# Graph attention and eight experts on one core: the first expert's first layer for all tokens, and expert blocks between the last graph loads

## What is computed

```python
x = x + gnn(layernorm(x), edges, ...)   # two attention layers over a graph: 8 heads of 768, then 1 head
h = layernorm(x)
probs = softmax(h @ Wg + bg)            # 8 experts
comb = one_hot(argmax(probs)) * max(probs)
y_e = gelu(h @ W1[e] + b1[e]) @ W2[e] + b2[e]      # 768 -> 3072 -> 768, for each e
ffn = sum_e comb[:, e] * y_e
v = clip(ffn @ Wv + bv, -3, 3)
scores = sigmoid(h @ Wm + bm); mask = scores >= 12th largest
gr, gi = diagonal of a complex tridiagonal inverse of v (two recursions over the tokens)
out = x + ffn + bk_scale * (clip([gr, gi] * mask) @ Wo + bo)
```

## Time and profile before

| | |
|---|---|
| runs | 503.71, 502.79, 503.6 us, median 503.6 |
| profiled execution, its own time | 506.07 us |
| its span in the trace | 504.3 us |
| granted TensorE clock, mean | 0.99 |
| busy TensorE / VectorE / ScalarE / GpSimd | 92% / 27% / 12% / 7% |
| bytes moved | 190.22 MB, mean 377 GB/s |

### The profile page before, as it was taken

One profiled execution on the slowest core, in us unless ns is written; L12 is line 12 of the kernel. 1 busy time (PEld: TensorE's weight loads), 2 busy tenths in 40 slices (PEclk: granted clock), 3 DMA queues, 4 the chain that ended last, 5 costly groups with the idle time before them and its releaser, 6 DMA issues.

```text
span 504.3 us, 6062 instructions
## 1 busy us (share of the span) xinstructions
PE 466.4 (92%) x2310; PEld 232.4 (46%) x2310; DVE 137.0 (27%) x362; ACT 60.6 (12%) x113; POOL 33.9 (7%) x52
## 2 busy tenths in 40 slices
PE   7999998999999999999999999998898889789892
PEld 5656665667558344344344353352243224224352
DVE  6573698426206311010010010020010002001165
ACT  1110212002003020021020020110020011002100
POOL 3262240000000000210000000000000000000000
PEclk9999999999999999999999999999999999999996
DMA  8889998898999999999999999999999999999700
GB/s 309 305 301 402 401 400 297 307 407 323 411 357 369 417 425 423 414 423 423 423 429 423 422 428 427 420 423 430 423 423 426 427 422 423 427 423 424 297 1 31
DMA packets 32541, 190.22 MB, mean 377 GB/s; under 512 B 5423, under 2 KB 5631, under 8 KB 18190
## 3 DMA queue, kind: packets, MB, share of 16 engines
q1 hardware_dynamic: 31694, 189.94, 92.6%
q0 software_dynamic: 544, 0.05, 0.1%
q10 hardware_dynamic: 288, 0.03, 0.0%
HBM read 189.62 MB, written 0.39 MB: 377 GB/s over the span
## 4 chain that ended last, share of the span: by engine, by line
PE 60%; SPq 16%; DMA 15%; DVE 5%; issue 2%; ACT 1%; POOL 0%; DVEq 0%
PE ps L1286 17%; PE ps L1259 16%; PE ps L1081 11%; SPq L337 8%; DMA chunk<-in_L_ffn_W 7%; DMA lower<-in_L_ffn_W 6%; PE ps L1041 6%; SPq L316 4%; SPq L332 3%; PE ps L1272 2%; PE ps L1069 2%; DMA slot<-in_L_gnn_W 2%; PE ps L1096 2%; PE ps L1221 2%; SPq L354 1%
## 5 line engine op out<-in xcount | busy, mean ns | idle before, releaser
L1286 PE MATMUL ps<-lower,hidden 128*64 128x384 f32 x600 | 102.9, 491 | 6.1 <-DMA lower<-in_L_ffn_W 6.1
L1259 PE MATMUL ps<-chunk,gathered 128*64 128x512 f32 x408 | 92.6, 597 | 10.0 <-DMA chunk<-in_L_ffn_W 10.0
L1286 PEld LDWEIGHTS ps<-lower,hidden 128*64 128x64 f32 x600 | 41.3, 136 | 58.3 <-issue 45.1
L1041 PE MATMUL ps<-slot,xT 128*128 128x384 f32 x192 | 64.1, 488 | 1.2 <-DMA slot<-in_L_gnn_W 1.2
L1259 PEld LDWEIGHTS ps<-chunk,gathered 128*64 128x64 f32 x408 | 27.5, 136 | 66.9 <-issue 47.6
L1081 PE MATMUL ps<-slot,eluT 128*128 128x384 f32 x168 | 55.3, 486 | 0.0
L866 DVE TENSOR_TENSOR biased<-ps,b_T 128x384 f32<-128x384 f32 x32 | 17.1, 554 | 133.5 <-PE ps L1272 133.5
L1041 PEld LDWEIGHTS ps<-slot,xT 128*128 128x128 f32 x192 | 35.6, 190 | 23.9 <-issue 1.3
L1259 PE MATMUL ps<-extra,gathered 128*64 128x512 f32 x168 | 38.9, 598 | 4.7 <-DMA extra<-in_L_ffn_W 4.6
L1081 PEld LDWEIGHTS ps<-slot,eluT 128*128 128x128 f32 x168 | 31.5, 190 | 20.7
L874 DVE TENSOR_SCALAR place_top<-slot_no,rank,small 128x128 f32<-128x128 f32 x8 | 2.8, 346 | 136.7 <-PE ps L1309 136.7
(11 more groups left out here) (288 smaller groups left out, 282.2 us busy)
## 6 DMA issues: line engine op xcount, KB each, us to landing
lower<-in_L_ffn_W SPq DMA_DIRECT2D x50, 1152.0 KB, 26.1
chunk<-in_L_ffn_W SPq DMA_DIRECT2D x34, 1536.0 KB, 22.7
slot<-in_L_gnn_W SPq DMA_DIRECT2D x31, 1152.0 KB, 12.7
extra<-in_L_ffn_W SPq DMA_DIRECT2D x14, 1536.0 KB, 27.7
lower_on<-in_L_ffn_W SPq DMA_DIRECT2D x14, 1152.0 KB, 30.9
slot<-in_L_gnn_W SPq DMA_DIRECT2D x3, 384.0 KB, 4.6
x_sb<-in_x SPq DMA_DIRECT2D x1, 384.0 KB, 3.4
out<-xc SPq DMA_DIRECT2D x1, 384.0 KB, 2.3
```

Source lines behind the costliest of these rows:

```text
L1041: last = T.matmul(ps[:, 2 * (h % 2) + b, 0:HB], xT[:, 3 * half + k, :], slots[n % RING][:, k, b * HB:(b + 1) * HB], start=(n % 2 == 0 and ...
L1259: last = T.matmul(ps[b * CAP:(b + 1) * CAP, s, 0:BANK], gathered[:, k, :], upper_homes[k][:, at:at + BANK], start=(k == 0), stop=(k == KT ...
L1286: last = T.matmul(ps[c * CAP:(c + 1) * CAP, 4, 0:HB], hidden[:, q, k, b, :], lower_homes[i][:, k, c * HB:(c + 1) * HB], start=(i == 0 and ...
```

## The change

It has two parts.

1. Loads. Expert 1's block 1 is issued after graph half 22, expert 0's blocks 2 and 0 after halves 23 and 24, expert 1's block 0 after half 25, and expert 0's block 1 after half 29. Block 5 moves ahead of block 10. For that, tensors get other places: `counts`, `mask_bias` and `att2_rows` leave the places of `extra0` and `extra1`, the last head's part of `eluT` gets its own place (`eluT_end`, reached by `elu_part`), and the rows of the second bias are spread before those of the second attention, whose spreading on GpSimd waits for the last activation. `load_round(1, 1, first=2)` loads only blocks 2 to 13.

2. The first expert's first layer is computed for all 128 tokens, before it is known which of them are its own: `first_up` multiplies `xT` (128 tokens, mean taken off, not yet scaled) by a block, six calls of 128x512 into six banks. The logits, rank, score, hot and bias products stand between the blocks. ScalarE and VectorE empty three banks each, scaled by `RSTD`, into the place of block 5 (`chunks[5]`), and `first_turn` gathers and turns at once by a product with `place_now`. The sixth mark of `used` in round 0 is then given by the first call of `down(0)`. The mean of x1 comes from a sum column (`HSUM`, one more product) and a base computed earlier; `centre_gate`, the first gather and the fillers WARM[5] to WARM[8] fall away. The other rounds are as before.

```diff
--- before.py
+++ after.py
@@ -138,27 +138,28 @@
...
+            [("gb2_rows", [P, 2, D]), ("stage_rows", [1, 2, D])],
             [("extra0", [P, HID])]])
         chunks_on = [extra0, extra1] + chunks[0:4]
         x1 = place("x1", [P, D])
-        xc, xT, upper = region([[("xc", [P, D]), ("xT", [P, KT, P])], [("upper", [P, WIDE])]])
-        xn = place("xn", [P, D])
-        (att_e, att_p, att_T, elu_y, elu_e, spare, h2_sb, wide_i, wide, gathered, biased, hidden, y_sb, place_now,
-         place_T) = region([
+        xc, xT, att2_rows, upper = region([[("xc", [P, D]), ("xT", [P, KT, P])], [("att2_rows", [P, 2, D])],
+                                           [("upper", [P, WIDE])]])
...
@@ -336,12 +332,9 @@
                     view = w2[e, at:at + HB, :].rearrange("(p k) c -> p k c", p=P)
                     sp.dma_start(lower_homes[i - CHUNKS][:, :, :], view).then_inc(landed[i], 16)
 
-            def load_round(r, e, second=False):
-                for i in range(LOADS):
-                    if second:
-                        second_room(i)
-                    else:
-                        sp.wait_ge(used, used_after(r - 1) + i + 1)
+            def load_round(r, e, first=0):
+                for i in range(first, LOADS):
+                    sp.wait_ge(used, used_after(r - 1) + i + 1 - first)
                     load(r, e, i, moe_in, chunks_on, lowers_on)
 
             for n in range(GNN_HALVES):
@@ -357,21 +350,32 @@
                         sp.dma_start(early_rows[0:1, :, j, :], vectors[0:EARLY, :].unsqueeze(0)).then_inc(early_in, 16)
                 if n == 5:
                     load_small()
-                if n == 27:
+                if n == 22:
+                    sp.wait_ge(spread, HEADS + 1)
+                    sp.wait_ge(bias_done, 1)
+                    sp.wait_ge(hot_ready, 4)
+                    load(1, 1, 1, moe_in, chunks_on, lowers_on)
+                if n == 23:
+                    sp.wait_ge(alpha_used, HEADS // 2)
+                    sp.wait_ge(agg_done, HEADS)
+                    load(0, 0, 2, lead_in, chunks, lowers)
+                if n == 24:
                     sp.wait_ge(alpha_used, HEADS)
                     load(0, 0, 0, lead_in, chunks, lowers)
-                if n == 30:
+                if n == 25:
                     sp.wait_ge(x_based, 1)
+                    load(1, 1, 0, moe_in, chunks_on, lowers_on)
+                if n == 29:
                     sp.wait_ge(used, 2 * HEADS + 6)
                     load(0, 0, 1, lead_in, chunks, lowers)
 
-            for i, consumed in ((6, 24), (7, 25), (2, 25), (3, 25), (8, 26), (9, 27), (10, 29), (4, 30), (11, 30),
-                                (5, 32), (12, 32), (13, 32)):
+            for i, consumed in ((6, 24), (7, 25), (3, 25), (8, 26), (9, 27), (5, 28), (10, 29), (4, 30), (11, 30),
+                                (12, 32), (13, 32)):
                 sp.wait_ge(used, consumed)
-                if i in (2, 3):
+                if i == 3:
                     sp.wait_ge(agg_done, 2 * HEADS)
                 load(0, 0, i, lead_in, chunks, lowers)
-            load_round(1, 1, second=True)
+            load_round(1, 1, first=2)
             with sp.Fori(2, ROUNDS) as r:
                 load_round(r, r)
...
@@ -418,13 +422,18 @@
                 if 2 <= i < HEADS:
                     pool.wait_ge(alpha_used, i - 1)
                 target = att_rows[:, i % 2, :, :] if i < HEADS else targets[i - HEADS][:, :, :]
-                n = 1 if i == HEADS + 1 else 2
+                if i == HEADS + 1:
+                    pool.wait_ge(elu_ready, 2 * HEADS)
+                n = 1 if i == HEADS else 2
                 G.partition_broadcast(target[:, 0:n, :].rearrange("p a c -> p (a c)"),
                                       places[i][:, 0:n, :].rearrange("p a c -> p (a c)")).then_inc(spread, 1)
                 following = {EARLY: (ATONCE, ATONCE + 1), ATONCE: (HEADS,)}.get(i, (i + 1,) if i >= HEADS else ())
                 for later_pair in following:
                     if later_pair < len(pairs):
                         pool.wait_ge(spread, i + 1)
+                        if later_pair == HEADS + 1:
+                            pool.wait_ge(used, 2 * HEADS)
+                            pool.wait_ge(alpha_used, HEADS)
                         fetch(later_pair, row_in)
 
...
@@ -506,19 +515,23 @@
 
             act.wait_ge(used, GNN_HALVES)
             act.wait_ge(dots2_done, 2)
-            S.copy(blocks(h2_sb[:, :]), ps[:, 0:2, 0:HB]).then_inc(h2_ready, 1)
+            S.activation(blocks(h2_sb[:, :]), ps[:, 0:2, 0:HB], ACT.Identity, accum_out=col(HSUM)).then_inc(h2_ready, 1)
             act.wait_ge(att_shift, 3)
             S.activation(att_p[:, 0, :], att_e[:, 0, :], ACT.Exp, bias=col(MX), scale=-1.0).then_inc(att_exp, 1)
+            act.wait_ge(mean2_ready, 1)
+            S.activation(x1[:, HB:D], x1[:, HB:D], ACT.Identity, bias=col(MEAN)).then_inc(base_half, 1)
             act.wait_ge(xT_done, 3)
-            S.copy(xT[:, 0:3, :].rearrange("p k t -> p (k t)"), ps[:, 5, 0:HB]).then_inc(xT_first, 1)
...
+                    act.wait_ge(place_turned, r + 1)
+                    S.copy(place_T[:, :], ps[:, 5, HB:512]).then_inc(place_T_ready, 1)
+
+                if first:
+                    for s in range(3):
+                        act.wait_ge(up_done, s + 1)
+                        S.activation(chunks[CHUNKS - 1][:, s * BANK:(s + 1) * BANK], ps[:, s, 0:BANK], ACT.Identity,
+                                     scale=col(RSTD)).then_inc(upper_ready, 1)
+                    gelu(0)
+                    gelu(1)
+                    turn_place()
+                    gelu(2)
+                    gelu(3)
+                    return
+                take_y(r)
+                turn_place()
                 for s in range(3):
                     take_upper(s)
...
@@ -768,19 +790,24 @@
             V.reciprocal(col(RS), col(SS))
             dve.wait_ge(att_turned, 3)
             V.tensor_copy(att_T[:, 0, :], ps[:, 4, P:2 * P]).then_inc(att_ready, 1)
...
-                                       accum_out=sums2[:, b:b + 1]).then_inc(x1_half, 1)
-            dve.wait_ge(x1_half, 2)
-            step(V.tensor_scalar(col(SUM), sums2[:, 0:1], sums2[:, 1:2], None, ALU.add))
-            V.tensor_scalar(col(MEAN), col(SUM), -1.0 / D, None, ALU.mult).then_inc(mean2_ready, 1)
-            dve.wait_ge(xT_done, 4)
-            V.tensor_copy(xT[:, 3:KT, :].rearrange("p k t -> p (k t)"), ps[:, 6, 0:HB]).then_inc(xT_second, 1)
+            step(V.tensor_scalar(col(SHARE), col(RS), -1.0 / D, None, ALU.mult))
+            dve.wait_ge(out2_sum, 1)
+            dve.wait_ge(base_ready, 1)
+            V.tensor_scalar(col(MEAN), ps[:, 7, 0:1], col(SHARE), col(BASE), ALU.mult,
+                            ALU.add).then_inc(mean2_ready, 1)
             dve.wait_ge(mean2_ready, 1)
+            step(V.tensor_scalar(x1[:, 0:HB], x1[:, 0:HB], col(MEAN), None, ALU.add))
+            for first, end in ((0, P), (P, HB), (HB, D)):
+                half = first // HB
+                dve.wait_ge(out2_done, half + 1)
+                if half:
+                    dve.wait_ge(base_half, 1)
+                V.scalar_tensor_tensor(out=x1[:, first:end], in0=ps[:, 2 + half, first - HB * half:end - HB * half],
+                                       scalar=col(RS), in1=x1[:, first:end], op0=ALU.mult,
...
@@ -821,20 +847,17 @@
             V.tensor_scalar(place_top[:, :], slot_no[:, :, :].rearrange("p a j -> p (a j)"), rank[:, 0:1],
                             col(TOPP), ALU.is_equal, ALU.mult).then_inc(top_ready, 1)
 
+            dve.wait_ge(x1_part, 3)
+            step(V.tensor_scalar(xn[:, :], x1[:, :], col(RSTD), None, ALU.mult))
+            V.tensor_scalar(x1[:, :], x1[:, :], col(MEAN), None, ALU.subtract).then_inc(xn_ready, 1)
+
...
+                if first:
+                    for s in range(3):
+                        dve.wait_ge(wide_done, s + 1)
+                        V.tensor_scalar(chunks[CHUNKS - 1][:, WIDE + s * BANK:WIDE + (s + 1) * BANK],
+                                        ps[:, 3 + s, 0:BANK], col(RSTD), None, ALU.mult).then_inc(wide_ready, 1)
+                    add_bias(0)
+                    add_bias(1)
+                    dve.wait_ge(turned, QU)
+                    next_place()
+                    add_bias(2)
+                    take_gathered(1, 5)
+                    take_threshold()
+                    add_bias(3)
...
@@ -1182,38 +1220,21 @@
             pe.wait_ge(alpha_used, HEADS + 1)
             T.matmul(ps[:, 4, 0:P], alpha2[:, 0, 1:2].to_broadcast([P, P]), ident[:, :], start=False,
                      stop=True).then_inc(att_scores, 1)
-            for k in range(KT):
-                last = T.matmul(ps[:, 6, 0:EXPERTS + 1], ones[:, :], gate_w[:, k, :], start=(k == 0),
-                                stop=(k == KT - 1))
-            last.then_inc(gate_sums, 1)
...
```

(101 more changed lines are left out.)

140 lines of the change are left out of this document (61 added, 79 removed).

## The result

The changed kernel takes 522.42 us (median of four runs, 520.70 to 522.87); the kernel before, on the same chip, 503.20 (502.52 to 503.71). The ratio is 1.036 [1.032, 1.039]: slower by 3.6%. The forecast was 514.1, the range ended at 518. So the direction and the path were right, and the size fell short by 8.3 us. The profiled execution took 522.87, its span 521.1.

A forecast was written before the change was run, and what follows sets the result against it. The stream of expert loads was taken as the bound, its end moving with the landing of (2,0), forecast 10.5 us later: span 504.3+10.5 = 514.8, put on the median as 514.1 us, range 510.5 to 518.

The forecast's parts named there:

- What bounds it: The stream of expert loads sets the end, which moves exactly as the landing of (2,0) moves.
- (2,0): Load of block 0 of expert 2; predicted issue 219.5, landing 226.7 against 216.2 before, +10.5 us.
- Part 1: Loads in other places and order: 14.5 us head start, gone by round 0; moving the broadcast costs nothing.
- Part 2: Routing removed between last aggregation and first layer: `first_up` starts at 158.8, a gain of 6.0 us.
- Part 3, the blocks: First layer for all 128 tokens: 5.16 us a block, six blocks 31.0 instead of 15.8, +15.2 us.
- rival A: Faster: a full-array 512-column call costs no more than a pair, 2.63 us a block; 498.9 us; chance 0.05.
- Rival B: The loads' head start counts whole: all 14.5 us stay, 489 us; chance 0.02.
- D: No change: effects cancel by chance or the program does not do as read, 503.6 us; chance 0.03.
- Part 3, the turns: Four `first_turn` groups in round 0, priced like the gather at 1.35 each: 5.4 us, before 2.0.
- rival C: Slower: granted clock falls once or twice around the start of `first_up`, 515.8 to 517.5 us; chance 0.12.
- The sum: Profiled span 504.3+10.5 = 514.8; that execution's 2.5 us over the median taken into account, 514.1 us.
- some engine carries extra work there: Reason given for adding 1 us to the landing of (2,0), which had landed 10.9 us after issue.

The follow-up runs named there:

- layer alone: The changed kernel with the loads in the order of before; 523.65 us, ratio to before 1.038.
- loads alone: The kernel before with only the change's new places and order of loads; 502.52 us against 504.06, ratio 0.998, and 0.997 when run again.
- half the columns: The changed kernel with 256 of 512 columns per call in blocks 1 to 5 of the all-token layer; 508.7 us, ratio to before 1.008.
- neighbouring columns: The changed kernel with first-round turns reading 128 neighbouring columns as weights instead of every third of 384; 517.5 us, ratio to before 1.025.

## Why the prediction was wrong, and where it was right

**What bounds it: right.** The end follows the issue of (2,0), which moves by 24 us, within 2 us over eleven profiles and within 3 over all twelve.

**Part 1: right.** Lead loads landed by 160.4 (predicted 159.3), and the head start was handed back at the wait for a free place, with the all-token layer (layer alone: nothing lost without it) and also without it (loads alone: (2,0) goes out no earlier by the order, 125.99 us after the same point). One term was put at nothing that is not nothing: the broadcast on GpSimd that the change moves had held up VectorE by 1.6 us in the graph stage. The prediction asked only whether the broadcast would be late for its reader, not whom it hindered where it stood.

**Part 2: right, and closer than it deserves.** Start of `first_up` 158.58, predicted 158.8. In the profile an aggregation that starts 1.2 earlier (154.67 for 155.82) and takes 1.0 longer at the lower clock (2.47 for 1.49) cancel; when run again the start is 157.03.

**Part 3, the blocks: right.** Six at 5.15 to 5.35, predicted 5.16; together 0.5 us over. The kernel with half the columns confirms that it is a price per column. So the page of the Trainium skill weighed in the prediction ("TensorE: Matmul & The Clock Gate", Back-to-back issue gap) gives half of what these f32 rows show (its formula has a floor for the smallest widths, which the prediction's "at any width" passes over; 384 and 512 columns lie above it), and rival A falls: it needed blocks below 3.4. Another page of the Trainium skill, "FP8 and Floating Point Precision" (TensorE Precision Notes), says that true FP32 takes four passes through the array; the row agrees, 5.25 us for six calls being 875 ns a call, four times 219. Rival B falls with the loads alone, D with the result.

**Part 3, the turns: the step that failed.** "`first_turn` is 12 instructions of 64 columns with 128-column weights, the shape of the gather, 1.29 each, 1.35 taken with its waits, four 5.4". The shape is the gather's, the access is not: the gather reads 128 neighbouring columns, `first_turn` every third one. The right row stood beside it: six transposes of the old turn, with the same step, in 0.89 us, 0.148 each; 48 of them are 7.1. At full clock the turns measured 8.15, 2.75 over the forecast of 5.4; neighbouring columns give 5.30. So the step costs 2.85, and even the better row would have been 1.0 short.

**The clock: rival C's kind, in another place and of another size.** It was put before `first_up`, behind gaps, as 1 to 2.7 us. It came inside the turns and the first two `down`s, where TensorE had no gap at all. In the profile it costs 8.86 + 9.55 − 8.15 − 7.89 = 2.4 us, and when run again 9.24 + 10.22 − 16.04 = 3.4. All six executions of the changed kernel have a mean clock of 0.979 to 0.982; those with neighbouring columns 0.987 and 0.989. "The granted clock is 1.00 in every stretch from 80 on" was true of one execution up to the tail, and of before it isn't always. The sum had nothing for the clock, and it is the second part of the miss.

The Trainium skill ("TensorE: Matmul & The Clock Gate", Part 1: The HAM clock gate) has the gate go by how busy TensorE has been, and gives the lower clock to its idle state. The stretches above do not agree: 2.00 busy of 2.00 on either side of the fall.

**The sum.** Issue of (2,0): 2.75 + 2.4 + 0.5 for the blocks + 0.2 for the gather (1.48 for 1.29), less about 0.6 in smaller items, among them a start of `first_up` 0.2 earlier: 5.2 (224.7 for 219.5). From there to the end 296.4 for a predicted 295.3: 1.1. That makes 6.3, the span of 521.1 against 514.8. The other 2.0 lie in the baseline: the profiled execution of before stood 2.9 us above its median of now, that of the changed kernel 0.4, so the spans moved by 16.8 and the medians by 19.2. So the 8.3 us are 2.75 of the turns, 2.4 of the clock, 2.0 of the baseline, 1.1 behind the issue and 0.1 of the rest. The first profile of before is the odd one in the table, with (2,0) landing 10.9 after issue and 299.0 to the end, where its second profile has 8.9 and 297.0; its surplus was carried over as if every kernel had it. The prediction's "some engine carries extra work there" is not tested; what makes that load late stays open. So does what in the turns brings the clock down: in the kernels without fillers the step of three and the fall came together (the one with half the columns fell too, 8.97 us of turns), and nothing separates the step from the length of time spent in the turns.

**The best version** is before with the loads' part alone: 502.5 us, 0.3% under before and 3.8% under the changed kernel. No run has the moved broadcast alone; by the chains it would have most of that gain. The all-token layer trades a gap of 6 us in the routing for 15.4 us more of blocks and 6 us more of turns.

## What to carry to other kernels

Find the mark that releases the unbroken part of a load stream and price every edit by what it does to that mark; a head start ahead of it is worth only what the free places can hold. Work put beside a gap costs all of it that is longer than the gap, so price its busy time first, here 31 us against a gap of 6. Take the duration from a row with the same access pattern and not only the same shape, and profile the baseline twice before carrying one execution's surplus onto a median. When an edit has several parts, compare the chains stretch by stretch before naming the part that gained: here 1.6 us came from a broadcast moved out of VectorE's way, and none from the reordering.

## What was not expected of the hardware

- f32 weights read with a step of three: 8.15 us for 48 instructions of `first_turn`, 0.170 each; neighbouring columns 5.30, 0.110 each, the rest of the instruction being the same.
- The granted clock fell from 2.4 to 1.2 GHz under a TensorE that was busy without a break, in small matmuls with 64 moving columns, and stayed there for 7 to 14 us.
- Whether the clock falls in the routing of the kernel before changes from one execution to the next, and with it 3 us of its time.
- A step of VectorE over 128x384 f32 that takes 0.35 us took 1.19 beside a broadcast of 1.25 us on GpSimd and 1.95 beside one of 2.01, ending 0.2 us after it each time.
